# A recurrence of 512 steps on one core: the low fp16 halves of its state products come from a scan over column triples instead of a subtraction

## What is computed

```
def step(h, xs):
    xzt, xrt, xht = xs
    z = sigmoid(xzt + h @ U_z + vz)
    r = sigmoid(xrt + h @ U_r + vr)
    hh = tanh(xht + r * h @ U + vh)
    h_new = (1.0 - z) * h + z * hh
    return (h_new, h_new)
```

## Time and profile before

| what | us |
|---|---|
| median of 3 runs | 3735.11 (3732.72 to 3735.58) |
| the profiled execution, its own time | 3734.91 |
| its span, first to last instruction | 3733.2 |
| the recurrence's steps, first to last `take1` | 2403.7 to 3452.9 |

### The profile page before, as it was taken

How to read it: one execution, slowest core, us unless ns; L and a number is a source line. 1 busy time by engine, 2 the same in 40 slices (tenths; PEclk the granted TensorE clock), 3 DMA queues, 4 the chain that set the end, 5 groups by cost and what they waited for, 6 DMA issues and landing times. The chain is left out here.

```text
span 3733.2 us, 108642 instructions
## 1 busy us (share of the span) xinstructions
PE 3208.2 (86%) x44394; PEld 2109.9 (57%) x44394; DVE 2112.1 (57%) x8196; ACT 1495.3 (40%) x4199; POOL 642.8 (17%) x361
## 2 busy tenths in 40 slices
PE   7798575898989895679984788899999999999899
PEld 3323342222323222578972334599999899999566
DVE  6312554555555533666648444377777777777554
ACT  3465542455555540477843122222222222222222
POOL 0000000466666671151210000000000000000000
PEclk8779787999999996789987899755555555555999
DMA  1000003000000004211120000100000000000000
GB/s 69 1 1 12 0 1 112 1 1 1 1 1 1 1 1 143 102 47 55 50 94 0 26 0 0 57 4 4 4 4 4 5 4 4 4 4 4 6 8 9
DMA packets 53375, 79.42 MB, mean 21 GB/s; under 512 B 11878, under 2 KB 43323, under 8 KB 51996
## 3 DMA queue, kind: packets, MB, share of 16 engines
q1 hardware_dynamic: 47504, 61.59, 5.0%
q0 software_dynamic: 3408, 9.34, 0.7%
q10 hardware_dynamic: 1988, 1.77, 0.2%
HBM read 56.01 MB, written 16.67 MB: 19 GB/s over the span
## 5 line engine op out<-in xcount | busy, mean ns | idle before, releaser
L1308 DVE TENSOR_REDUCE diff_mx<-diff_m_ps 128x1 f32<-128x512 f32 x512 | 329.9, 686 | 330.2 <-PE diff_m_ps L1158 330.2
L2773 PE MATMUL gru_sums<-gru_take,gru_u 128*128 128x4 f16 x12288 | 479.8, 167 | 4.4 <-issue 3.7
L2773 PE MATMUL gru_sums<-gru_keep,gru_u 128*128 128x4 f16 x12288 | 471.3, 166 | 1.3
L2773 PEld LDWEIGHTS gru_sums<-gru_take,gru_u 128*128 128x128 f16 x12288 | 432.8, 105 | 4.7 <-issue 3.7
L2773 PEld LDWEIGHTS gru_sums<-gru_keep,gru_u 128*128 128x128 f16 x12288 | 410.8, 104 | 14.8 <-issue 1.5
L1262 ACT ACTIVATE diff_probs<-diff_s_ps 128x512 f32<-128x512 f32 x512 | 277.9, 595 | 225.0 <-PE diff_s_ps L1152 225.0
L1152 PE MATMUL diff_s_ps<-diff_qk 32*128 32x512 f32 x1024 | 294.9, 649 | 63.7 <-DVE diff_mx L1308 56.1
L2773 PE MATMUL gru_sums<-gru_rh,gru_u 128*128 128x4 f16 x6144 | 279.6, 170 | 27.5 <-DVE gru_rh L2842 4.6
L1158 PE MATMUL diff_m_ps<-diff_qk 32*128 32x512 f32 x1024 | 293.5, 650 | 6.4 <-DVE diff_mx L1308 6.4
L1354 POOL TENSOR_TENSOR diff_sums<-diff_sums,diff_probs 128x2048 f32<-128x2048 f32 x64 | 289.3, 4520 | 32.0 <-ACT diff_probs L1262 31.8
L2773 PEld LDWEIGHTS gru_sums<-gru_rh,gru_u 128*128 128x128 f16 x6144 | 237.3, 107 | 69.9 <-DVE gru_rh L2842 6.6
(11 more groups left out here) (486 smaller groups left out, 5660.1 us busy)
## 6 DMA issues: line engine op xcount, KB each, us to landing
moe_weights<-in_L_ffn_W SPq DMA_DIRECT2D x16, 1024.0 KB, 13.0
expert_slots<-diff_blank SPq DMA_DIRECT2D x1, 5031.0 KB, 21.1
stream_a<-expert_slots SPq DMA_DIRECT2D x39, 129.0 KB, 2.1
moe_weights<-in_L_cond_w_R SPq DMA_DIRECT2D x1, 4096.0 KB, 14.8
moe_both<-expert_pairs SPq DMA_DIRECT2D x4, 1024.0 KB, 9.6
stream_b<-in_x SPq DMA_DIRECT2D x4, 512.0 KB, 8.1
hyp_wf<-in_L_cond_w_f SPq DMA_DIRECT2D x2, 1024.0 KB, 8.5
stream_b<-in_xT SPq DMA_DIRECT2D x1, 2048.0 KB, 12.5
```

The costliest lines, as they stand in the source:

```text
L1308: dve.tensor_reduce(mx[:, i % 2, kt, at:at + 1], m_ps[:, m % 3, :], X_AXIS, ALU.max).then_inc(ph.maxes_ready, 1)
L2773: last = pe.matmul(sums[:, par, g, m * B:(m + 1) * B], part[:, g, c, m * P:(m + 1) * P], state[:, c * B:(c + 1) * B], start=False, stop=(l ...
```

## The change

Only the recurrence changes, and there only DVE's instructions, the layout of some tiles, and waits. PE's and ACT's lists stay the same but for the tiles that they read and write.

The low half of rh and of take is no longer made from an fp32 copy. Instead, tiles of triples hold, for each of the 8 columns, three factors (0, 1, r) and three parts (a, b, rh1), and one `tensor_tensor_scan` over the 24 elements runs state = factor·state - part. It starts each triple at -a, goes to -a - b, and ends at r·(-a - b) - rh1. With a + b = -h, kept as an fp16 high and low half, the last element is r·h - rh1, the low half. For take the factors are (0, 1, hh) and the parts (a, b, take1), with a + b = -1024·z.

What goes: the fp32 product of rh (L2843) and the two subtractions (L2845, L2859). The fp32 product of take stays, since h needs it. What comes: two scans (`rest_of`, L2832); two instructions that split -1024·z (L2861, L2865), between the keep instructions; two that split -h (L2879, L2883), behind h. The tile of the high halves and of the factors has a stride of 3 elements, and r and hh are written into it by ACT.

Waits: the instruction that writes `rh1` waits for `before_ready` (the split of -h) and for `r_ready`, in that order of the code; the one that writes `take1` for `weigh_ready` (the split of -1024·z) and then for `hh_ready`; L2883 for `h_ready` and then for `high_ready`.

```diff
-        r = ph.sb("r", [P, N])
+        r_factors = ph.sb("r_factors", [P, N, 3])
+        r_parts = ph.sb("r_parts", [P, N, 3], F16)
+        rh_rests = ph.sb("rh_rests", [P, N, 3], F16)
+        hh_factors = ph.sb("hh_factors", [P, N, 3])
+        hh_parts = ph.sb("hh_parts", [P, N, 3], F16)
+        take_rests = ph.sb("take_rests", [P, N, 3], F16)
+        one_of = lambda tile, k: tile[:, :, k]
+        r, rh1, rh2 = one_of(r_factors, 2), one_of(r_parts, 2), one_of(rh_rests, 2)
+        hh, take1, take2 = one_of(hh_factors, 2), one_of(hh_parts, 2), one_of(take_rests, 2)
...
+                def rest_of(out, factors, parts):
+                    pairs = lambda tile: tile[:, :, :].rearrange("p n k -> p (n k)")
+                    return dve.tensor_tensor_scan(pairs(out), pairs(factors), pairs(parts), 0.0, ALU.mult, ALU.subtract)
...
+                        dve.wait_ge(ph.before_ready, t + 1)
                         dve.wait_ge(ph.r_ready, t + 1)
-                        dve.tensor_tensor(rh1[:, :], r[:, :], before, ALU.mult).then_inc(ph.rh1_ready, 1)
-                        dve.tensor_tensor(rh[:, :], r[:, :], before, ALU.mult).then_inc(ph.rh_ready, 1)
-                        dve.wait_ge(ph.rh_ready, t + 1)
-                        dve.tensor_tensor(rh2[:, :], rh[:, :], rh1[:, :], ALU.subtract).then_inc(ph.rh2_ready, 1)
+                        dve.tensor_tensor(rh1, r, before, ALU.mult).then_inc(ph.rh1_ready, 1)
+                        dve.wait_ge(ph.rh1_ready, t + 1)
+                        rest_of(rh_rests, r_factors, r_parts).then_inc(ph.rh2_ready, 1)
...
+                        dve.wait_ge(ph.z_ready, 2 * t + 2)
+                        dve.tensor_scalar(one_of(hh_parts, 0), z[:, :], -SCALE, None, ALU.mult).then_inc(ph.high_ready, 1)
...
+                        dve.wait_ge(ph.high_ready, 2 * t + 1)
+                        dve.scalar_tensor_tensor(out=one_of(hh_parts, 1), in0=z[:, :], scalar=-SCALE, in1=one_of(hh_parts, 0),
+                                                 op0=ALU.mult, op1=ALU.subtract).then_inc(ph.weigh_ready, 1)
+                        dve.wait_ge(ph.weigh_ready, t + 1)
                         if s % KEPT == 0:
                             dve.wait_ge(ph.kept, COPIES * i + (s // KEPT + 1))
                         dve.wait_ge(ph.hh_ready, t + 1)
...
+                        dve.wait_ge(ph.take1_ready, t + 2)
+                        rest_of(take_rests, hh_factors, hh_parts).then_inc(ph.take2_ready, 1)
                         dve.wait_ge(ph.take_ready, t + 1)
-                        dve.tensor_tensor(take2[:, :], take[:, :], take1[:, :], ALU.subtract).then_inc(ph.take2_ready, 1)
                         dve.tensor_tensor(h[:, s, :], take[:, :], keep[:, :], ALU.add).then_inc(ph.h_ready, 1)
+                        dve.scalar_tensor_tensor(out=one_of(r_parts, 0), in0=take[:, :], scalar=-1.0, in1=keep[:, :], op0=ALU.mult,
+                                                 op1=ALU.subtract).then_inc(ph.high_ready, 1)
                         dve.wait_ge(ph.h_ready, t + 2)
+                        dve.wait_ge(ph.high_ready, 2 * t + 2)
+                        dve.scalar_tensor_tensor(out=one_of(r_parts, 1), in0=h[:, s, :], scalar=-1.0, in1=one_of(r_parts, 0),
+                                                 op0=ALU.mult, op1=ALU.subtract).then_inc(ph.before_ready, 1)
```

More of the change, by code:

```diff
@@ L2642, in recurrence @@
         (ph.dve_step, ph.pe_done, ph.act_read, ph.h_ready, ph.r_sums, ph.z_sums, ph.hh_sums, ph.r_ready,
-         ph.z_ready, ph.rh1_ready, ph.rh_ready, ph.rh2_ready, ph.keep1_ready, ph.keep_ready, ph.keep2_ready, ph.take1_ready,
-         ph.take_ready, ph.take2_ready, ph.hh_ready, ph.kept, ph.inputs_ready) = ph.semaphores(
+         ph.z_ready, ph.rh1_ready, ph.before_ready, ph.rh2_ready, ph.keep1_ready, ph.keep_ready, ph.keep2_ready, ph.take1_ready,
+         ph.take_ready, ph.take2_ready, ph.hh_ready, ph.kept, ph.inputs_ready, ph.high_ready, ph.weigh_ready) = ph.semaphores(
             "dve_step", "pe_done", "act_read", "h_ready", "r_sums", "z_sums", "hh_sums", "r_ready",
-            "z_ready", "rh1_ready", "rh_ready", "rh2_ready", "keep1_ready", "keep_ready", "keep2_ready", "take1_ready",
-            "take_ready", "take2_ready", "hh_ready", "kept", "inputs_ready")
+            "z_ready", "rh1_ready", "before_ready", "rh2_ready", "keep1_ready", "keep_ready", "keep2_ready", "take1_ready",
+            "take_ready", "take2_ready", "hh_ready", "kept", "inputs_ready", "high_ready", "weigh_ready")
         N, KEPT, S = DC * B, KEPT_AT_ONCE, STEPS_IN_BODY
@@ L2662, in recurrence @@
         keep2 = ph.sb("keep2", [P, N], F16)
-        take1 = ph.sb("take1", [P, N], F16)
-        take2 = ph.sb("take2", [P, N], F16)
-        r = ph.sb("r", [P, N])
+        r_factors = ph.sb("r_factors", [P, N, 3])
[7 more added lines that the diff above has]
+        hh, take1, take2 = one_of(hh_factors, 2), one_of(hh_parts, 2), one_of(take_rests, 2)
         z = ph.sb("z", [P, N])
         rest = ph.sb("rest", [P, N])
-        rh = ph.sb("rh", [P, N])
-        rh1 = ph.sb("rh1", [P, N], F16)
-        rh2 = ph.sb("rh2", [P, N], F16)
-        hh = ph.sb("hh", [P, N])
         keep = ph.sb("keep", [P, N])
@@ L2818, in _ @@
                         act.wait_ge(ph.hh_sums, t + 1)
-                        act.activation(hh[:, :], sums[:, par, C_, 0:N], ACT.Tanh, scale=undo_c
+                        act.activation(hh, sums[:, par, C_, 0:N], ACT.Tanh, scale=undo_c
                                        ).then_inc(ph.hh_ready, 1)
@@ L2832, in _ @@
                 dve.memset(keep2[:, :], 0.0).then_inc(ph.keep2_ready, 1)
-                dve.memset(take1[:, :], 0.0).then_inc(ph.take1_ready, 1)
-                dve.memset(take2[:, :], 0.0).then_inc(ph.take2_ready, 1)
+                for tile in (r_factors, hh_factors):
+                    dve.memset(one_of(tile, 0), 0.0)
+                    dve.memset(one_of(tile, 1), 1.0)
+                dve.memset(r_parts[:, :, :], 0.0).then_inc(ph.before_ready, 1)
+                dve.memset(hh_parts[:, :, :], 0.0).then_inc(ph.take1_ready, 1)
+                dve.memset(take_rests[:, :, :], 0.0).then_inc(ph.take2_ready, 1)
                 dve.memset(h[:, S - 1, :], 0.0).then_inc(ph.h_ready, 1)
@@ L2853, in _ @@
                         dve.wait_ge(ph.hh_ready, t + 1)
-                        dve.scalar_tensor_tensor(out=take1[:, :], in0=hh[:, :], scalar=SCALE, in1=z[:, :], op0=ALU.mult,
+                        dve.scalar_tensor_tensor(out=take1, in0=hh, scalar=SCALE, in1=z[:, :], op0=ALU.mult,
                                                  op1=ALU.mult).then_inc(ph.take1_ready, 1)
-                        dve.scalar_tensor_tensor(out=take[:, :], in0=hh[:, :], scalar=SCALE, in1=z[:, :], op0=ALU.mult,
+                        dve.scalar_tensor_tensor(out=take[:, :], in0=hh, scalar=SCALE, in1=z[:, :], op0=ALU.mult,
                                                  op1=ALU.mult).then_inc(ph.take_ready, 1)
+                        dve.wait_ge(ph.take1_ready, t + 2)
+                        rest_of(take_rests, hh_factors, hh_parts).then_inc(ph.take2_ready, 1)
                         dve.wait_ge(ph.take_ready, t + 1)
-                        dve.tensor_tensor(take2[:, :], take[:, :], take1[:, :], ALU.subtract).then_inc(ph.take2_ready, 1)
                         dve.tensor_tensor(h[:, s, :], take[:, :], keep[:, :], ALU.add).then_inc(ph.h_ready, 1)
+                        dve.scalar_tensor_tensor(out=one_of(r_parts, 0), in0=take[:, :], scalar=-1.0, in1=keep[:, :], op0=ALU.mult,
+                                                 op1=ALU.subtract).then_inc(ph.high_ready, 1)
                         dve.wait_ge(ph.h_ready, t + 2)
+                        dve.wait_ge(ph.high_ready, 2 * t + 2)
+                        dve.scalar_tensor_tensor(out=one_of(r_parts, 1), in0=h[:, s, :], scalar=-1.0, in1=one_of(r_parts, 0),
+                                                 op0=ALU.mult, op1=ALU.subtract).then_inc(ph.before_ready, 1)
                         inputs(bass.ds(t + 2 if s < S - 2 else (t + 2) % T, 1), par)
```

2 lines of the change are left out of this document (1 added, 1 removed).

## The result

| kernel | median us (range) | ratio to before (95% interval) |
|---|---|---|
| before | 3733.91 (3705.91 to 3735.58) | |
| after | 3795.36 (3771.2 to 3797.47) | 1.016 (1.0118 to 1.0201) |

The sign and the range of the prediction held. The change of +61 us is twice the forecast +31, and 3795 lies above the forecast's own bounds, 3745 to 3791. The profiled execution of after took 3795.94 us by its own time, 61.0 more than that of before.

A forecast was written before the change was run, and what follows sets the result against it. The prediction took a dependency ring of 2.03 us a step, not PE's throughput, as the bound; 2 x (0.07 - 0.08 + 0.04) = +0.06 us over 512 steps added 31 us to 3734.9, giving 3766, range 3738 to 3800.

The forecast's parts named there:

- ring of six pieces: One recurrence step, r through `rh1`, `rh2`, hh, `take1`, `take2` to the next r: 2.03 us with no slack.
- second ring: Through rest, `keep1` and PE's loads to those with `take2`: 0.05 us shorter than the ring of six pieces.
- Part 1: At both low halves: waiting for the high half instead of the fp32 copy saves 0.08 us, twice a step.
- Part 2: At both low halves: a scan of 24 elements takes 0.21 us instead of the subtraction's 0.17, +0.04 twice a step.
- second rival: At the low halves: the scan takes 0.18 to 0.19 us, so no change that can be told, 3735 to 3742; chance 0.10.
- Part 3: At `rh1` and `take1`: the gate's wait, written last, becomes an instruction of its own, +0.07 us at each, every step.
- first rival: At `rh1` and `take1`: the separate wait costs nothing, so the kernel gets faster, 3709 us; chance 0.10.
- Part 4: On DVE: the four split instructions fit into waiting time; -1024·z's split is seen 0.14 us early, -h's 0.18.
- third rival: Behind the second scan: each instruction starts only when the one ahead has ended, 0.15 us a step more, 3843; chance 0.08.
- Part 5: Over the recurrence: 2 x (0.07 - 0.08 + 0.04) = +0.06 us a step, 31 us over 512 steps.

The follow-up runs named there:

- covered: split_early without the waits for `weigh_ready` and `before_ready`, and with L2883 no longer waiting for `h_ready`; 3695.87 us, ratio 0.992 to before.
- long_scan: covered with 16 columns of triples instead of 8, so each scan runs over 48 elements; 3744.82 us, ratio 1.006 to before.
- before_two_waits: The kernel before with an early-met wait written ahead of each gate wait, at `rh1` and `take1`; 3816.84 us, ratio 1.026.
- gates_first: The changed kernel with the gate's wait written first at both `rh1` and `take1`; 3770.12 us, ratio 1.0115 to before.
- split_early: gates_first with the split of -1024·z moved up: high half behind `keep1`, low half behind keep, `keep2` last; 3744.18 us, ratio 1.0023 to before.

## Why the prediction was right, and what it mis-sized

*What bounds the kernel.* The ring of six pieces held: in after they are 2 x (0.182 + 0.102 + 0.208 + 0.208 + 0.361) = 2.122 for a measured 2.120. That they add up to the step proves nothing, since they follow one another; what shows the ring is that the last piece, from the low half's end to the next r or hh, stays at 0.359 to 0.364 in all twelve kernels while the others change. The second ring was put at 0.05 under the first, and covered came to 1.986, 0.047 under 2.033. PE's loads there show that the two rings have all but met: the first load with the low half of take still starts 0.053 behind the scan's end, as in after, so the first ring ends last; but it stands only 0.031 behind the last load with `take1`, where loads in an unbroken row stand 0.0275 apart. No run goes below that, so the bound itself is not tested.

*Part 1, the fp32 products: mis-sized.* Forecast -0.08, measured 0.279 to 0.208, which is -0.071. The high half now takes 0.174 and not the 0.168 of the row I used, because it is written with a stride; the rest is rounding of rows with two digits. The same stride makes r and hh 0.005 longer, a term that the sum did not have. The change shows the stride of 3 in its tiles; I gave it no price.

*Part 2, the scan: right.* Forecast 0.21, measured 0.208. The slope of double an element's cost, taken from scans of 512, was confirmed by long_scan. The second rival, a scan of 0.18 to 0.19, falls.

*Part 3, the lone wait: right.* Forecast +0.07 twice, measured 0.102 - 0.032 = 0.070 twice, and shown apart from everything else by before_two_waits. The wait written last is the one that stands alone, 512 times at both lines. The first rival falls. That an instruction that waits on several engines may have a wait put ahead of it, as the Trainium skill says on the page Perfetto Trace Analysis, section Identifying Dependency Chains, agrees with the rows; its price here is 0.070 us.

*Part 4, the covers: right for this kernel.* The forecast laid out from r's start `rh1` 0.27, scan 0.47, hh 1.04, `take1` 1.32, second scan 1.52, next r 2.09; the timeline has 0.29, 0.50, 1.07, 1.36, 1.56, 2.13. The split of -1024·z had the slack it was given, and the split of -h a little more. h starts 0.13 behind the start of a scan of 0.21, so the third rival's flush did not come. The Trainium skill, on the page VectorE: DVE Perf Modes, section The DRAIN you can't avoid, has the next op wait for the pipe to empty but says that one which is not held starts earlier. The row agrees with that exception, and not with the wait. gates_first showed what the cover was made of: take the gate's lone wait away, and the split becomes the bound.

*Part 5, the sum.* Per half it was 0.07 - 0.08 + 0.04 = 0.03. Measured, it is 0.070 - 0.071 + 0.041 + 0.005 = 0.045, so 0.09 a step where the medians have 0.087 and the forecast had 0.06. That is 14 of the missing 30 us. The other long steps, 12.5 us, had no term at all: I priced DVE's added instructions where they stand, and not for being more. So the mechanism on the ring was right, and the size was missed by two terms put at nothing, the stride and the long steps, besides the rounding. The last 4 us lie ahead of the recurrence.

## What to carry to other kernels

Of two waits ahead of an instruction, write first the one that is met last: here the other order cost 0.07 us at each place, although the other wait was long met. It helps in full only if the other is met some 0.07 us before it (split_early). Better still, ask whether the second wait is needed, since a wait that some later consumer already makes on the same engine may cover it; that turned 1.6% slower into about 0.5% faster. A cover should be checked again after each gain, since a gain can take away the very gap that hid something.
